# Attention projections by eights: queries of eight heads in one beat, their keys in the next, with the batch's preparation further ahead

## The chip, the cores and the metric

The kernel runs on one core of a Trainium2 chip (trn2). Its engines are TensorE (PE), VectorE (DVE), ScalarE (ACT), GpSimd (POOL) and SyncE (SP), which issues most of the DMAs. The metric is the device time of one execution in microseconds, the median of three runs. One further execution was profiled; all rows below come from it.

## The reference, cut to what matters

Sixteen batches of 256 rows with 128 features pass through one layer: layer norm, then attention and a mixture of experts side by side, both added to the input.

```python
xn = layernorm(x)                                   # (16, 256, 128)
kv_c = rms(xn @ W_kv) * g_kv;  q_c = xn @ W_q       # ranks 32 and 64
q = concat(heads(q_c @ W_qdec), rope(heads(q_c @ W_qrope)))    # 16 heads of 8 + 32
k = concat(heads(kv_c @ W_kdec), rope(heads(xn @ W_krope)))
v = heads(kv_c @ W_vdec)
attn = softmax(causal(q @ k.T / sqrt(40)))
y = (attn @ v) @ W_o
probs = softmax(xn @ Wg)                            # 8 experts, two per row
moe = sum over the two picked e of weight * (silu(xn @ W1[e] + b1[e]) @ W2[e] + b2[e])
shared = 0.1 * (silu(xn @ Ws1 + bs1) @ Ws2 + bs2)
out = x + y + moe + shared
```

## The kernel before, in words

The order of the work is written out by hand. Each engine runs its own copy of the same loop over beats t and four steps s (`beats`, line 466), from FIRST = -5 to LAST = 71. A group g is four heads of a batch (HG = 4, PER = 4 groups to a batch, NG = 64 groups), and beat t starts group t. What an engine does in a step is decided by lags: `project(t)` in step 0, the transposes ("turnings") of its parts from one to two beats later (`TURN_AT`, line 48), scores for the maximum three beats later, the negated maxima four, the scores for the softmax five, values six. Engines wait for each other through semaphores only, and every queue is in order.

One beat, in its parts:

- `project(g)` on TensorE (line 1411) fills both banks of the tensor "projections": for each of the two row tiles j two matmuls of 160 columns for the queries of four heads (lines 1428, 1429), three of 128 columns for the rope part of the keys (1433 to 1435) and two of 32 columns for key content and values (1436, 1437): 14 matmuls. Before it, it waits for the preparation of the beat before, since that uses the same banks.
- `rotate(g)` on VectorE (1034) multiplies by the cosine table and makes two products with the sine table (1038, 1042, 1043); `add_turned` on GpSimd (693, line 697) adds them; `part_heads` on ScalarE (820, line 825) writes the high part twice; `take_low` on GpSimd (699, line 702) the low part.
- `turn_parted` (1441, line 1448) turns the parts in four units of four transposes; `put_stack` copies each unit to QK, on VectorE for i = 1 (1050) and on ScalarE otherwise (802).
- `scores_for_max` (1452, lines 1461 to 1464), `head_max` on VectorE (1057), `negative_max` on VectorE (1060, lines 1067, 1071, 1073), `turn_maxima` on TensorE (1473), `put_max` on ScalarE (810), `place_maxima`, a DMA of SyncE's queue (521).
- `head_scores` (1477), `exponential` on ScalarE (796), `group_values` (1490); per pair of groups `turn_pair` and `norm_pair`, per batch the output projection.

Scores for the maximum, transposes, maxima and outputs share a ring of three PSUM banks; the units' order (`units_at`, 98) fixes which bank each takes, and TensorE may fill a unit only when the one three places before it was read.

A batch's preparation runs in four of the beats ahead of its first group: `normalise` (beat -5 relative to it), `turn_rows` and its copies (-4), `small_rows` and `small_products` (-3), `small_stacks` (-2), `turn_stacks` and its copies (-1). TensorE's parts stand at the end of step 2, ScalarE's copies in step 3 behind part_heads (lines 857, 862, 867, 868), VectorE's share (lines 1308, 1011 to 1021, 1027 to 1032) in steps 2 and 3. The router works on four batches at a time (`ROUTE_AT`), its rows are scattered to expert order by GpSimd's indirect DMAs (`scatters_at`, line 740), and `list_blocks` on VectorE (1167) lists the expert blocks in the last beats. SyncE meanwhile zeroes free rows (`fill`, 542) and loads the shared weights (`load_shared`, 552). Behind the beats follow 31 passes of experts (`hidden`, `activate`, `expert_out`); the first two and the last six are the shared expert's, and the third is the first that turns routed rows (1590).

```python
                if s == 3 and group(t):
                    part_heads(t)
                b = batch_at(t, -4)
                if s == 3 and b is not None:
                    ...
                    act_f(xhl[:, b % 2, 0, :], banks[0][:, 0:T], ACT.Copy).then_inc(s_xh, 1)
```

## Time and profile before

| What | us |
|---|---|
| median of 3 runs | 987.04 |
| lowest and highest run | 982.11, 991.94 |
| the profiled execution | 989.52 |
| its span in the profile | 987.8 |

The span runs from the first to the last recorded instruction; what lies around it is in the execution's own time. In the profile's rows an engine's name is followed by the line of the kernel, the operation, and output<-input. PE is TensorE's matmuls and PEld its weight loads, which overlap them. "PEclk" is the granted TensorE clock as a share of full speed, a mean over the window. "x4" after a row stands for four instructions merged into one. A name in angle brackets tells what ended an idle time.

### The profile page before, as it was taken

How to read it: one execution, taken by the hardware profiler on the slowest of the kernel's cores; microseconds unless marked ns; L12 is line 12 of the kernel's file. 1: busy time of each engine (PE TensorE's matmuls, PEld its weight loads, DVE VectorE, ACT ScalarE, POOL GpSimd, SP SyncE). 2: the span in 40 equal slices, each digit the busy share in tenths (PEclk: the TensorE clock that was granted, in tenths of full speed). 3: DMA queues.
4: the chain of work that ended last, by engine and by line, in shares of the span. 5: the costliest groups of instructions: out<-in, count | busy, mean ns of one | idle time of the engine just before them, and what ended most of it. 6: DMA issues, size and time to landing. Idle time of an engine off the chain costs nothing.

```text
span 987.8 us, 17323 instructions
## 1 busy us (share of the span) xinstructions
PE 796.4 (81%) x5926; PEld 691.3 (70%) x5926; DVE 636.4 (64%) x1546; ACT 512.6 (52%) x1006; POOL 385.0 (39%) x346
## 2 busy tenths in 40 slices
PE   2688888888878788887888888789556999988974
PEld 2677787777768677776777777687444888876863
DVE  4456577665747876565777657469565777765775
ACT  2335454545654454555546456556334777765562
POOL 3534333445545454434434334334610000246544
PEclk9999777778978897888879789778866999998988
DMA  6020211102020211100011100000234477877643
GB/s 177 12 76 1 76 41 37 57 31 82 7 84 7 82 53 38 61 7 21 7 39 42 39 18 8 21 7 11 76 109 148 141 243 245 247 220 231 210 120 83
DMA packets 51557, 79.43 MB, mean 80 GB/s; under 512 B 5889, under 2 KB 31470, under 8 KB 51470
## 3 DMA queue, kind: packets, MB, share of 16 engines
q1 hardware_dynamic: 46798, 69.23, 22.1%
q0 software_dynamic: 4096, 8.40, 2.9%
q8 instruction: 49, 0.80, 0.4%
q10 hardware_dynamic: 576, 0.69, 0.2%
q14 instruction: 38, 0.31, 0.1%
HBM read 47.82 MB, written 29.88 MB: 79 GB/s over the span
## 4 chain that ended last, share of the span: by engine, by line
PE 59%; DVE 15%; ACT 9%; issue 8%; another core or an unknown queue 3%; POOL 2%; DMA 2%; SPq 1%; ACTq 0%; POOLq 0%; DVEq 0%
PE bank L1448 7%; ACT heads_parted L825 5%; PE bank L1670 5%; PE projections L1608 4%; PE bank L1608 4%; PE bank L1484 4%; PE bank L1498 3%; PE bank L1487 3%; PE bank L1464 3%; PE bank L1461 3%; PE bank L1674 2%; PE projections L1428 2%; POOL QK L758 2%; PE projections L1433 2%
## 5 line engine op out<-in xcount | busy, mean ns | idle before, releaser
L1057 DVE TENSOR_REDUCE mx<-bank 128x3 f32<-128x384 f32 x256 | 141.9, 555 | 106.7 <-PE bank L1464 86.1
L697 POOL TENSOR_TENSOR rot<-rot,t 128x512 f32<-128x512 f32 x64 | 82.0, 1282 | 269.3 <-DVE t L1043 269.3
L796 ACT ACTIVATE prob<-bank 128x384 f32<-128x384 f32 x256 | 125.8, 492 | 91.2 <-PE bank L1487 80.4
L1448 PE MATMUL bank<-identr,heads_parted 128*120 128x128 f32 x1024 | 158.4, 289 | 8.9 <-DVE mx L1057 7.2
L802 ACT ACTIVATE QK<-bank 120x512 fp32r<-120x512 f32 x192 | 115.0, 599 | 61.0 <-PE bank L1448 53.8
L758 POOL DMA_INDIRECT QK<-expert_outs,out_at x64 | 67.6, 1056 | 190.4 <-DMA expert_outs<-prob 166.9
L702 POOL TENSOR_TENSOR heads_parted<-rot,heads_parted 128x640 fp32r<-128x640 f32 x64 | 98.9, 1545 | 96.5 <-ACT heads_parted L825 96.1
L1448 PEld LDWEIGHTS bank<-identr,heads_parted 128*120 128x120 f32 x1024 | 126.6, 159 | 11.3 <-DVE mx L1057 6.9
L810 ACT ACTIVATE mT<-bank 8x256 fp32r<-8x256 f32 x64 | 23.8, 372 | 206.3 <-PE bank L1473 195.8
L1461 PE MATMUL bank<-QK 120*128 120x256 f32 x256 | 110.5, 432 | 8.2 <-ACT mT L810 6.6
L1357 DVE TENSOR_TENSOR QK<-vaug,QK 128x512 fp32r<-128x512 f32 x124 | 85.5, 695 | 46.8 <-ACT QK L910 37.6
L1484 PE MATMUL bank<-QK 122*128 122x256 f32 x256 | 105.3, 411 | 4.5 <-DMA QK<-mT 4.5
L1428 PE MATMUL projections<-wqa,qsT 128*128 128x160 f32 x128 | 38.3, 321 | 85.3 <-DVE wb L1308 30.0
L1050 DVE CAST QK<-bank 120x512 fp32r<-120x512 f32 x64 | 44.0, 688 | 78.3 <-PE bank L1448 76.6
L1428 PEld LDWEIGHTS projections<-wqa,qsT 128*128 128x128 f32 x128 | 26.8, 210 | 93.8 <-issue 65.3
L1487 PE MATMUL bank<-identb,mask_qk 128*128 128x256 bf16 x256 | 85.7, 335 | 0.0
L1464 PE MATMUL bank<-mask_qk,identb 128*128 128x256 bf16 x256 | 85.2, 333 | 0.0
L825 ACT ACTIVATE heads_parted<-rot 128x1280 fp32r<-128x1280 f32 x64 | 80.8, 1263 | 1.8 <-POOL rot L697 1.8
L1461 PEld LDWEIGHTS bank<-QK 120*128 120x128 f32 x256 | 64.1, 250 | 10.5 <-ACT mT L810 6.8
L740 POOL DMA_INDIRECT expert_rows<-xn,place_of x64 | 65.5, 1023 | 12.6 <-issue 11.8
L1484 PEld LDWEIGHTS bank<-QK 122*128 122x128 f32 x256 | 59.1, 231 | 8.8 <-DMA QK<-mT 4.7
L1462 PE MATMUL bank<-QK 120*128 120x128 f32 x256 | 64.2, 251 | 0.0
(227 smaller groups left out, 2038.2 us busy)
## 6 DMA issues: line engine op xcount, KB each, us to landing
...
```

The costliest lines, as they stand in the source:

```text
L702: nc.gpsimd.tensor_tensor(low_of(g), rotated(g), high_of(g), ALU.subtract).then_inc(s_lo, 1)
L758: nc.gpsimd.indirect_dma_start(out=gy[:, t, k, :], out_offset=None, in_=outs_d[0:READY[q] * SLOTS, :], in_offset=bass.IndirectOffsetOnAxis ...
L796: act_f(prob[:, g % 2 * HG + n, :], ST_PS[n % 2][:, 0:3 * P], ACT.Exp, scale=SCALE).then_inc(s_exp, 1)
L802: act_f(stacked(g, i), B_PS[bank_of(k)][0:KQ, :].rearrange("p (h t) -> p h t", h=HG), ACT.Copy)\
L825: act_f(high_of(g, 2), rotated(g).unsqueeze(3).to_broadcast([P, 2, NT * HG, 2, D]), ACT.Copy).then_inc(s_hi, 1)
L1057: V.tensor_reduce(mx[:, 0:3, g % 2 * HG + n], B_PS[bank_of(k)][:, 0:3 * P].rearrange("p (a c) -> p a c", a=3), AX.X, ALU.max).then_inc(s_b ...
L1357: V.tensor_tensor(aparts[:, m % 2, 1, c, :], act[c], high, ALU.subtract).then_inc(s_alo, 1)
L1448: ins = nc.tensor.transpose(B_PS[bank_of(k)][0:KQ, n * P:(n + 1) * P].bitcast(F32R), parted(g, i, n), identr[:, :])
L1461: mm(ps[:, 0:T], q[:, P:T], kk, start=True, stop=False, skip_group_check=True)
L1464: mm(diag, identb[:, :], mask_qk[:, :].unsqueeze(1).to_broadcast([P, 2, P]), start=False, stop=True, skip_group_check=True).then_inc(s_bfi ...
L1484: mm(ps[:, P:3 * P], k[:, 0:P], q, start=True, stop=False, skip_group_check=True)
L1487: mm(diag, mask_qk[:, :], identb[:, :].unsqueeze(1).to_broadcast([P, 2, P]), start=False, stop=True, skip_group_check=True).then_inc(s_st, 1)
```

## The change

A beat now projects one side for eight heads. Beat g with g even makes the queries of the eight heads of groups g and g+1, beat g+1 their keys and values. `PH` is 8; the rotation works on two tiles of eight heads and not on four of four heads; the parts of queries (high, high, low) and keys (low, high, high) are laid out by the parity of g. Scores need both beats, so they start at step 14 behind a group's beat and not 12, the maxima at 18 and not 16, the scores for the softmax at 22 and not 20, the values half a beat later. A batch's preparation is moved to beats -7, -6, -4, -3 and -2, its TensorE parts all in beats of queries (even beats), with a third slot for the batch's rows and a second for its turned keys. On ScalarE the copies of the preparation go ahead of the stack copies in step 3, and part_heads to step 0 of the next beat. On VectorE the rotation is split around the maxima. On GpSimd take_low goes to step 1, the scatters to step 0 and two beats earlier, with waits on the scores from beat 63 on; the weight splits to step 3. In the last beats the shared loads are split over beats 66 and 68, the fills of free rows follow them, and the listing's last part goes to the fourth expert pass. The first expert's hidden layer starts two beats ahead of the last beat and not one.

```diff
-OS = 2 * T // 2
-ROW = HG * D
-MAX_LAG, NEG_LAG, SC_LAG, PV_LAG = 3, 4, 5, 6
+PH = 2 * HG
+ROW = PH * D
+MAX_AT, NEG_AT, SC_AT = 14, 18, 22
 TURN_AT = {3: (1, 0), 0: (2, 1), 1: (2, 2), 2: (2, 3)}
-FIRST, LAST = -5, NG + 7
-HL_SLOTS = 3
-HL_SIDE = 1040
-HL_SLOT = 2000
-P_SLOTS = 2 * HG
+FIRST, LAST = -7, NG + 7
+HL_SLOTS, X_SLOTS, P_SLOTS = 3, 3, 2 * HG
+HL_SLOT = NT * PH * KQ
...
+def staged(t, s, at):
+
+    g, n = divmod(STEPS * t + s - at, HG)
+    return (g, n) if group(g) else (None, n)
...
+def values_at(t, s):
+
+    if s == 0 and group(t - 7) and (t - 7) % 2 == 0:
+        return t - 7
+    if s == 2 and group(t - 6) and (t - 6) % 2 == 1:
+        return t - 6
...
-ROUTE_AT = {0: (10, 3), 1: (11, 3), 2: (12, 2), 3: (12, 3), 4: (13, 2), 5: (14, 0), 6: (14, 3)}
-POS_AT = 14
+ROUTE_AT = {0: (9, 2), 1: (10, 1), 2: (10, 3), 3: (11, 1), 4: (11, 3), 6: (12, 3), 5: (13, 2)}
+EXP_AT, POS_AT = 10, 12
...
-    if 15 <= t < 63:
-        return (t - 15) // 16, ((t - 15) % 16,)
-    if 63 <= t < 71:
-        return GROUPS - 1, (2 * (t - 63), 2 * (t - 63) + 1)
+    if 13 <= t < 61:
+        return (t - 13) // 16, ((t - 13) % 16,)
+    if 61 <= t < 69:
+        return GROUPS - 1, (2 * (t - 61), 2 * (t - 61) + 1)
...
+                if (t, s) == (66, 0):
+                    load_shared(0)
+                if (t, s) == (68, 0):
+                    load_shared(1)
+                    sp.wait_ge(s_free, 1)
+                    for i in range(E):
                         fill(sp.value_load(fill_row[0:1, i:i + 1], min_val=0, max_val=ROWS - SLOTS))
...
-                if s == 0 and group(t - 1):
+                if s == 1 and group(t - 1):
                     take_low(t - 1)
...
+                q, picks = scatters_at(t) if s == 0 else (None, ())
                 for pick in picks:
+                    if t >= 63:
+                        pool.wait_ge(s_st, STEPS * t - SC_AT + 2 * (pick % 2))
...
+                first = 8 * (g % PER // 2)
+                for odd in range(2):
+                    act_f(vaug[:, g // PER % V_SLOTS, :, first + odd:first + PH:2, 2 * DC * odd:2 * DC * odd + DC],
+                          prs[:, :, ROW:ROW + PH * DC].rearrange("p j (n a d) -> p j n a d", a=2, d=DC)[:, :, :, odd, :],
+                          ACT.Copy).then_inc(s_v, 1)
...
+                g, n = staged(t, s, SC_AT)
+                if g is not None:
+                    exponential(g, n)
+                b = batch_at(t, -6)
+                if s == 3 and b is not None:
+                    sc.wait_ge(s_afill, rows_turned(b))
+                    at_least(sc, s_xst[b % X_SLOTS], 16 * (b // X_SLOTS))
+                    at_least(sc, s_pfill, PER * (b - X_SLOTS + 1))
+                    act_f(xhl[b % X_SLOTS][:, 0, :], banks[0][:, 0:T], ACT.Copy).then_inc(s_xh, 1)
+                b = batch_at(t, -4)
+                if s == 3 and b is not None:
+                    sc.wait_ge(s_afill, small_done(b))
+                    at_least(sc, s_small, b)
+                    act_f(smt[:, :, :], banks[1][:, :].rearrange("p (j c) -> p j c", j=NT)[:, :, 0:SMW],
+                          ACT.Copy).then_inc(s_smh, 1)
+                b = batch_at(t, -2)
+                if s == 3 and b is not None:
+                    sc.wait_ge(s_afill, stacks_turned(b))
+                    at_least(sc, s_pfill, PER * b - 1)
+                    act_f(qsT[:, :, :], banks[1][:, 0:T].rearrange("p (j t) -> p j t", j=NT), ACT.Copy).then_inc(s_smT, 1)
+                    act_f(ksT[b % 2][:, :, :], banks[1][0:3 * RKV, T:2 * T].rearrange("p (j t) -> p j t", j=NT),
+                          ACT.Copy).then_inc(s_smT, 1)
+                if s == 0 and group(t - 1):
+                    part_heads(t - 1)
                 lag, i = TURN_AT[s]
                 if group(t - lag) and i != 1:
                     put_stack(t - lag, i)
-                if s == 2 and group(t):
+                if s == 2 and group(t) and t % 2:
                     read_values(t)
-                if s == 1 and pair_at(t) is not None:
+                if s == 3 and pair_at(t) is not None:
                     pair = pair_at(t)
...
+                if s == 1 and group(t):
+                    rotate(t)
+                g = begun(t, s, NEG_AT)
+                if g is not None:
+                    negative_max(g)
...
+                g, n = staged(t, s, MAX_AT)
+                if g is not None:
+                    head_max(g, n)
+                if s == 1 and group(t):
+                    rotate_turned(t)
+                lag, i = TURN_AT[s]
+                if group(t - lag) and i == 1:
+                    put_stack(t - lag, i)
...
+                if m == 3:
+                    next(listing, None)
...
+                b, first = g // PER, 8 * (g % PER // 2)
+                heads = slice(first, first + PH)
                 at_least(pe, s_turned, g)
-                at_least(pe, s_v, g)
-                x_next, s_next = batch_at(g - 1, -4), batch_at(g - 1, -3)
-                if x_next is not None:
-                    pe.wait_ge(s_xl, x_next + 1)
-                if s_next is not None:
-                    pe.wait_ge(c_a, s_next * SMALL_STEPS + 7)
+                at_least(pe, s_v, g // 2 * 2)
+                b_x, b_s, b_k = (batch_at(g - 1, beat) for beat in (-6, -4, -2))
+                if b_x is not None:
+                    pe.wait_ge(s_xl, b_x + 1)
+                if b_s is not None:
+                    pe.wait_ge(c_a, b_s * SMALL_STEPS + 7)
+                if b_k is not None:
+                    pe.wait_ge(s_smT, 2 * (b_k + 1))
+                if g == 0:
+                    pe.wait_ge(s_smT, 2)
+                    pe.wait_ge(s_xl, 2)
                 if group_at(g - 1, POS_AT) is not None:
                     pe.wait_ge(s_posr, group_at(g - 1, POS_AT) + 1)
                 for j in range(NT):
                     ps = prs[:, j, 0:ROW]
-                    mm(ps, qsT[:, j, :], wqa[:, heads, :], start=True, stop=False, skip_group_check=True)
-                    mm(ps, qsT[:, j, :], wqb[:, heads, :], start=False, stop=True, skip_group_check=True)
-                for j in range(NT):
-                    ps = prs[:, NT + j, 0:ROW].rearrange("p (h d) -> p h d", d=D)
-                    xh, xl = (xhl[:, b % 2, a, j * P:(j + 1) * P] for a in range(2))
+                    if g % 2 == 0:
+                        mm(ps, qsT[:, j, :], wqa[:, heads, :], start=True, stop=False, skip_group_check=True)
+                        ins = mm(ps, qsT[:, j, :], wqb[:, heads, :], start=False, stop=True, skip_group_check=True)
+                        continue
+                    ps = ps.rearrange("p (h d) -> p h d", d=D)
+                    xh, xl = (xhl[b % X_SLOTS][:, a, j * P:(j + 1) * P] for a in range(2))
                     mm(ps[:, :, DC:D], xh, wkr[:, 0, heads, :], start=True, stop=False, skip_group_check=True)
                     mm(ps[:, :, DC:D], xh, wkr[:, 1, heads, :], start=False, stop=False, skip_group_check=True)
                     mm(ps[:, :, DC:D], xl, wkr[:, 0, heads, :], start=False, stop=True, skip_group_check=True)
-                    mm(ps[:, :, 0:DC], ksT[:, j, :], wkv[:, 0, heads, :], start=True, stop=True, skip_group_check=True)
-                    ins = mm(prs[:, NT + j, ROW:ROW + HG * DC], ksT[:, j, :], wkv[:, 1, heads, :],
+                    mm(ps[:, :, 0:DC], ksT[b % 2][:, j, :], wkv[:, 0, heads, :], start=True, stop=True, skip_group_check=True)
+                    ins = mm(prs[:, j, ROW:ROW + PH * DC], ksT[b % 2][:, j, :], wkv[:, 1, heads, :],
                              start=True, stop=True, skip_group_check=True)
                 ins.then_inc(s_pfill, 1)
...
-                if s == 0 and group(t):
-                    project(t)
+                g, n = staged(t, s, SC_AT)
+                if g is not None:
+                    head_scores(g, n)
+                g, n = staged(t, s, MAX_AT)
+                if g is not None:
+                    scores_for_max(g, n)
                 lag, i = TURN_AT[s]
                 if group(t - lag):
                     turn_parted(t - lag, i)
-                g = t - PV_LAG
-                if group(g) and s == (0 if g % 2 else 2):
-                    group_values(g)
-                if s == 0 and group(t - NEG_LAG):
-                    turn_maxima(t - NEG_LAG)
-                if s == 2 and pair_at(t) is not None:
-                    turn_pair(pair_at(t))
+                if values_at(t, s) is not None:
+                    group_values(values_at(t, s))
+                if s == 0 and group(t):
+                    project(t)
+                g = begun(t, s, NEG_AT)
+                if g is not None:
+                    turn_maxima(g)
                 if s == 1 and out_batch(t) is not None:
                     turn_normed(out_batch(t))
+                if s == 2:
+                    if batch_at(t, -2) is not None:
+                        turn_stacks(batch_at(t, -2), t)
+                    if batch_at(t, -4) is not None:
+                        small_rows(batch_at(t, -4), t)
+                    if batch_at(t, -6) is not None:
+                        turn_rows(batch_at(t, -6), t)
+                    if group_at(t, POS_AT) is not None:
+                        count_places(group_at(t, POS_AT), t)
+                if s == 3 and pair_at(t) is not None:
+                    turn_pair(pair_at(t))
                 if s == 3 and out_batch(t) is not None:
                     output_projection(out_batch(t))
-                if s == 2:
-                    if batch_at(t, -4) is not None:
-                        turn_rows(batch_at(t, -4), t)
-                    if batch_at(t, -3) is not None:
-                        small_rows(batch_at(t, -3), t)
-                    if batch_at(t, -1) is not None:
-                        turn_stacks(batch_at(t, -1), t)
-                    if group_at(t, POS_AT) is not None:
-                        count_places(group_at(t, POS_AT), t)
-                if (t, s) == (LAST - 1, 0):
+                if (t, s) == (LAST - 2, 0):
```

The parts left out change the slices with the slots (`parted`, `high_of`, `low_of`, `stacked`), count the fillings of the preparation's banks, and make the cosine and sine tables for eight heads. GpSimd's two powers and SyncE's store of the rows follow the preparation's new beats.

## Rows read from the trace of the kernel before

**Rows 1.** The page, part 1: busy time and share of each engine.
```profile
PE 796.4 (81%) x5926; PEld 691.3 (70%) x5926; DVE 636.4 (64%) x1546; ACT 512.6 (52%) x1006; POOL 385.0 (39%) x346
```

**Rows 2.** Windows: busy us (instructions) of each engine, PEclk, DMA share, GB/s.
```profile
302.00:696.00 394.00, 325.92 (x2890) 289.91 (x2890) 263.13 (x688) 208.93 (x436) 166.35 (x137) 0.85 0.09 29
696.00:761.10 65.10, 36.27 (x278) 27.42 (x278) 36.05 (x79) 21.61 (x46) 18.23 (x18) 0.71 0.38 122
761.10:987.80 226.70, 201.45 (x949) 163.14 (x947) 156.61 (x304) 142.41 (x238) 67.56 (x64) 0.95 0.62 191
```

**Rows 3.** VectorE's rotation, line 1038: durations min/median/max, first and last start.
```profile
L1038 DVE TENSOR_TENSOR rot<-projections,rope_table x64: 811/814/825, 22.0 to 696.0; 128x640 f32<-128x640 f32 x64
```

**Rows 4.** Waits from 302 to 696: us in total, times, longest.
```profile
PE projections L1428 <- DVE wb L1308: 15.9, 8, 2.0
PE projections L1428 <- DVE smt L1011: 15.7, 8, 2.0
PE projections L1428 <- ACT ksT L868: 15.3, 9, 1.7
```

**Rows 5.** Timeline, all engines, from 454.6: start, us, what, [idle before <-releaser].
```profile
454.65 0.98 POOL L740 DMA_INDIRECT expert_rows<-xn,place_of  x1 [0.15 <-issue]
...
455.10 1.26 ACT L825 ACTIVATE heads_parted<-rot 128x1280 fp32r<-128x1280 f32 x1
456.25 0.38 ACT L857 ACTIVATE wb<-projections 128x256 fp32r<-128x256 f32 x1
456.45 1.54 POOL L702 TENSOR_TENSOR heads_parted<-rot,heads_parted 128x640 fp32r<-128x640 f32 x1 [0.82 <-ACT heads_parted L825]
456.52 0.49 ACT L796 ACTIVATE prob<-bank 128x384 f32<-128x384 f32 x1
456.66 0.42 DVE L1308 TENSOR_TENSOR wb<-projections,wb 128x256 fp32r<-128x256 f32 x1 [1.78 <-ACT wb L857]
...
457.23 0.31 PE L1428 MATMUL projections<-wqa,qsT 128*128 128x160 f32 x1 [1.99 <-DVE wb L1308]
```

**Rows 6.** Windows behind the idle time of rows 5, and near 708.
```profile
457.20:462.80 5.60, 5.57 (x43) 4.64 (x43) 2.31 (x5) 0.55 (x2) 0.79 (x1) 0.58 0.14 47
706.00:709.00 3.00, 1.87 (x27) 1.31 (x26) 1.33 (x3) 0.00 (x0) 2.39 (x3) 1.00 0.39 119
```

**Rows 7.** Timeline of TensorE from 480.09: scores, then one projection, then four turnings.
```profile
480.09 0.36 PE L1461 MATMUL bank<-QK 120*128 120x256 f32 x1
480.30 0.22 PE L1462 MATMUL bank<-QK 120*128 120x128 f32 x1
...
480.40 0.32 PE L1428 MATMUL projections<-wqa,qsT 128*128 128x160 f32 x1
...
481.97 0.52 PE L1448 MATMUL bank<-identr,heads_parted 128*120 128x128 f32 x4
```

**Rows 8.** Windows: two beats, each from one rotation to the next.
```profile
474.90:485.10 10.20, 9.78 (x98) 8.34 (x96) 6.82 (x19) 5.72 (x13) 3.91 (x3) 0.82 0.03 9
485.10:494.80 9.70, 7.54 (x62) 7.00 (x61) 6.96 (x25) 5.79 (x14) 4.59 (x4) 0.87 0.02 8
```

**Rows 9.** Lines 1071 and 697: durations in ns min/median/max, first and last start.
```profile
L1071 DVE TENSOR_SCALAR nhl<-mx x64: 170/172/1575, 51.4 to 737.0; 128x8 fp32r<-128x8 f32 x64
...
L697 POOL TENSOR_TENSOR rot<-rot,t x64: 1262/1282/1297, 23.6 to 697.5; 128x512 f32<-128x512 f32 x64
```

**Rows 10.** Timeline of VectorE near 19: the normalised rows of batch 1.
```profile
19.02 0.60 DVE L1002 TENSOR_SCALAR xn<-xres,mv,rstd 128x128 f32<-128x128 f32 x2 [0.44 <-POOL rstd L722]
```

**Rows 11.** The chain that ended last, from 708 to 766: start, us, what.
```profile
708.81 14.43 another core or an unknown queue
...
738.16 5.99 DMA QK<-mT
...
746.63 2.46 issue
```

**Rows 12.** The first long operation of the listing's last part.
```profile
L1269 DVE TENSOR_TENSOR xn<-xn 128x2048 f32<-128x2048 f32 x1 | 2.3, 2292 | 0.0
```

249 lines of the change are left out of this document (110 added, 139 removed).

## The prediction, made before the change was run

> **What bounds the kernel now.** I read the page's engine line first, then the windows by stage, then the waits, then the timeline. The page shows TensorE busiest at 81% and VectorE at 64% [rows 1]; neither is full, so the end is set by how they wait for each other. The windows divide the span [rows 2]: beats up to the last rotation at 696.0, the last beats to the first turning of routed rows at 761.1, then 226.7 us of experts, in which TensorE is busy 201.45 us and of which the change touches one place.
>
> The rotation runs once per beat, 64 times from 22.0 to 696.0, so 63 beats take 674.0 us, 10.70 each [rows 3]. The window from 302 to 696 holds 394/10.70 = 37 of them, 10.65 us each. Per such beat the window gives TensorE 325.92/37 = 8.81 us busy, VectorE 263.13/37 = 7.11, ScalarE 5.65, GpSimd 4.50, at a granted clock of 0.85 [rows 2].
>
> In three beats of four TensorE stands still before `project`: 15.9 + 15.7 + 15.3 = 46.9 us in 25 waits, 1.88 us each, 1.27 per beat over 37 [rows 4]. The timeline shows why: ScalarE starts part_heads (1.26 us) at 455.10, copies the batch's rows behind it at 456.25, VectorE subtracts at 456.66, and TensorE, idle since about 455.24, projects at 457.23 [rows 5]. The wait is paid twice: in the 5.6 us behind it the granted clock is 0.58, mostly the lower level of 1.2 GHz, whereas from 706 to 709, with TensorE busy only 1.87 of 3 us, it is still 1.00, that is 2.4 GHz [rows 6].
>
> **The change part by part.**
> (1) Preparation ahead of part_heads. ScalarE's copies of rows, small products and turned stacks now stand directly behind the exponential of step 3, and part_heads goes to step 0 of the next beat. `project` also moves behind the turning of step 0 and, in even beats, the values. Between the preparation's matmuls and the next `project` lie now two steps of score and turning work; three matmuls of scores take 0.31 us, twice a step, four turnings 0.4 to 0.5 [rows 7], about 1 us a step at full clock. The chain that must fit is ScalarE's exponential 0.49, copy 0.38, VectorE 0.42 [rows 5], about 1.5 us with hand-overs. It fits, so I take the whole 1.27 us per beat as gone (bounds: 0 and 1.27).
> (2) The clock. 0.85 means that 30% of the 394 us, 118 us, ran at half clock. At full clock the busy part (83%) of that would take half: 49 us less, 1.3 per beat. Bounds: 0, if other waits of the same size come, and 1.3.
> (3) Wide projections. A beat's 14 matmuls start between 480.40 and 481.97, 0.112 us apart whatever their width, so two beats cost 3.14 us; 256 columns take 0.21 [rows 7]. Afterwards two beats issue 4 of 320 columns, 6 of 256 and 4 of 64. With every one at 0.112 that is 1.57 us; with the wide ones at 0.22, 0.21 and the narrow at 0.112, 2.59. I take 2.0, nearer the per-instruction price since 128 and 160 columns showed no difference: 0.57 us less per beat (0.28 to 0.79).
> TensorE's side of a beat would be 10.65 - 1.27 - 1.3 - 0.57 = 7.5 us.
> (4) VectorE keeps all its work: one rotation of 640 and two products of 256 elements per partition, the same maxima, the same preparation in larger lumps. Its 7.11 us per beat now weigh as much as TensorE. It cannot be full: rotate stands first in step 1 and waits for a later `project`. The two windows between rotations give the price of such coupling: from 485.1 to 494.8 took 9.7 us with VectorE busy 6.96; without the 1.7 us wait for the stacks 8.0, 1.04 above its busy time [rows 4, 8]. So 7.11 + 1.04 = 8.15.
> (5) negative_max moves from step 0 to step 2, directly behind the products whose end starts GpSimd's sum of 1.28 us. Its small operations are sometimes held: L1071 has a median of 172 ns and a maximum of 1575 [rows 9]. TensorE's turn_maxima and the maxima behind wait for it. I add 0.35 us per beat (bounds 0 and 1.3) and come to 8.5 us.
> The Trainium skill bears on this (SBUF — State Buffer, "Who interferes with whom"): VectorE and GpSimd share one port pair, and a VectorE operation with two SBUF inputs waits out a GpSimd operation that reads SBUF and came first. The maximum of 1575 ns agrees with a lock held for a whole GpSimd operation. It speaks against the new place of negative_max; what it would do is rival 2.
> (6) Same cost, other place: read_values becomes two ScalarE copies in every second beat, each of the old size; the second ksT and third x slot cost no instruction; the router's parts and the scatters come one to two beats earlier; take_low is now behind the scatter on GpSimd, which puts 0.98 us of descriptor work ahead of it [rows 5], and ahead of add_turned. GpSimd has 6.1 us free per beat of 10.65, 4.0 of 8.5. From the part copy (1.26) and take_low (1.54) to the turning in step 3 some 5 us of TensorE's steps remain against 2.8 plus the exponential of step 0. I cost it at nothing; rival 4 is its exposure.
> (7) Start. Batch 1's rows are now prepared ahead of the first `project`. Before, its xn came only at 19.02 [rows 10], 3 us ahead of the first rotation; now it, its turning, copy and subtraction stand in front of ScalarE's copies for that projection: at most the 3 us, half of it made good by a shorter first projection: +1.5 (0 to 3).
> (8) Last beats. 65.1 us from 696.0 to 761.1. The chain there has one piece of 14.43 us put to an unknown queue, 5.99 of the maxima's rows landing, 2.46 before the values [rows 11]. In the first, GpSimd issued its last scatters without a pause (two per beat in the program, but nothing held them); the rows' DMA started in the midst of 2 MB of loads; the third waited behind the listing on VectorE. The change paces the scatters by the scores, starts the loads at beats 66 and 68 around the last place_maxima, moves the listing's last part away, and lets TensorE start the first expert's hidden layer a beat earlier in place of a wait. I take off 14.4, 4.0 (2 us is a transfer's own) and 2.5, and add 3 for the half beat by which scores and values come later: 47.2 us. Fills, loads and rows behind beat 68 are about 4.5 MB; at the experts' stage rate of 191 GB/s over a share of 0.62, 308 GB/s, 15 us, from about 27 us on: 42, just inside. Bounds for the stretch: 40 and 65.
> (9) The listing's last part, three operations like L1269 with 2.29 us and some small ones, 7.5 us [rows 12], now falls into expert pass 3. VectorE is busy 156.61 of 226.7 us there, 2.0 us free per pass of 6.5; I take 3 us exposed (0 to 7.5).
>
> **Sum.** First rotation 22.0 + 1.5 = 23.5; eight first beats at 9.5 us (clock and pipeline still filling) 76; 55 at 8.5, 467.5: last rotation at 567.0, 129 us earlier. Then 47.2, 226.7 and 3: a span of 843.9. The profiled execution lasted 989.52 for its span of 987.8, 1.7 more, and 2.5 above the median 987.04; so 843.9 + 1.7 - 2.5 = 843 us.
>
> **The rivals.**
> 1. VectorE and TensorE overlap better than the old windows show: 7.5 us a beat, the sum of (1) to (3). 55 us less: 788. For it: TensorE no longer stops; against: VectorE would have 95% of the beat.
> 2. The port. GpSimd's sum is released by the same products that negative_max follows, so its three small operations wait about 1.28 us each beat, TensorE's turn_maxima with them, and part of the clock loss returns: 9.4 us a beat, 50 more: 893. For it rows 9; against: the first small operation is in before GpSimd starts, and in the old order most were not held.
> 3. The waits were only one of several causes. From 474.9 to 485.1, a beat with no such wait, still took 10.2 us at a clock of 0.82 [rows 8]. If beats stay at 9.9, 77 more: 920. Against: that low clock was left by the wait before it.
> 4. Slower than before: the later part_heads. If ScalarE's burst in step 3 and GpSimd's scatter and weight splits push take_low past the turning of step 3, TensorE waits each beat. Exposed by half, 1.4 us, and the clock falling as in rows 6 (5.6 us at 0.58, some 2.4 us lost): 3.8 us a beat, 209 more: 1052. It decides from 144/55 = 2.6 us per beat.
> 5. The change doesn't do what it says: the wide matmuls cost per column what two narrow ones did, and the preparation's wait only moves to the next queue: within 1% of before.
>
> **How the numbers follow.** Forecast (beats of 7.9 to 9.1 us, 810 to 876) 0.55; rival 1 0.13; rival 2 0.18; rival 3 0.07; rival 4 0.04; rival 5 0.03. The range of 8 in 10 takes the forecast, the nearer part of rival 1 and rival 2 with a longer tail of last beats: 800 to 915. Faster by over 1%, about what a measurement of this kernel can tell from none: 0.93; within 1%: 0.03; slower: 0.04.
>
> **What would show it.** (1) right: no idle of over 1 us before the first projection line, wrong if the row copy on ScalarE still ends behind it. (2) a granted clock of 0.95 or more over the steady beats. (3) four matmuls of 320 columns starting about 0.15 us apart. (4) rotations 8.5 us apart and VectorE busy over 80% of such a window. (5) the median of what is now L1071 near its 172 ns; a median over a microsecond is rival 2. (8) under 50 us from the last rotation to the first turning of expert rows, and no 14 us piece. (9) one gap of about 3 us in pass 3 or 4. The prediction is wrong if GpSimd's chain shows as TensorE's longest wait at the turning, or the clock stays at 0.85.

## The result, and the profile after

The changed kernel takes 916.69 us (median of four, 907.99 to 919.31), the kernel before 989.49 in the same set: a ratio of 0.9259, 95% interval 0.9176 to 0.9343. That is 7.4% faster. The forecast was 843 us, range 800 to 915. Half of the forecast gain came. Ratios here and below are computed from the executions in the faster of two states, so they are not exactly the quotients of the medians. The profiled execution of the changed kernel took 915.65 us for a span of 913.9.

The page, part 1, of the changed kernel, to be held against [rows 1]:

```profile
PE 712.7 (78%) x5478; PEld 618.1 (68%) x5478; DVE 664.2 (73%) x1546; ACT 514.7 (56%) x1006; POOL 384.9 (42%) x346
```

TensorE is busy 84 us less with 448 fewer matmuls. VectorE, with not one instruction more (1546 as before), is busy 28 us longer: some of its instructions got slower. This is the first sign of the cause.

The windows and the rotation answer to [rows 2] and [rows 3]; the columns are as there.

```profile
235.00:630.20 395.20, 305.26 (x2873) 273.15 (x2871) 295.33 (x736) 230.29 (x476) 184.09 (x154) 0.89 0.11 35
630.20:690.70 60.50, 41.83 (x320) 33.77 (x320) 33.08 (x76) 25.21 (x53) 14.89 (x14) 0.75 0.34 109
690.70:913.90 223.20, 201.71 (x948) 162.96 (x948) 164.43 (x313) 141.57 (x237) 68.37 (x64) 0.96 0.64 198
```
```profile
L1083 DVE TENSOR_TENSOR rot<-projections,rope_table x64: 809/824/826, 25.6 to 630.2; 128x640 f32<-128x640 f32 x64
```

Read: 604.6 us for 63 beats, 9.60 each (before 10.70; forecast 8.5 after the first eight). The last beats, up to the first turning of routed rows, take 60.5 us (before 65.1, forecast 47.2), the experts 223.2 (before 226.7, forecast 229.7). Against the forecast the last rotation is 63.2 us late, the last beats are 13.3 us longer and the experts 6.5 shorter: the span of 913.9 misses 843.9 by 70. A steady beat has 305.26/41.2 = 7.4 us of TensorE, so TensorE stands still for 2.2 us, and VectorE has 295.33/41.2 = 7.2.

What TensorE waits for in that window, longest first (us, times, longest), where [rows 4] had three waits ahead of `project`:

```profile
PE bank L1534 <- DVE nhl L1121: 62.9, 40, 3.3
PE bank L1570 <- ACT heads_out L909: 18.3, 19, 1.0
PE bank L1522 <- DVE mx L1105: 4.2, 8, 0.5
```

The waits ahead of `project` are gone. In their place stands one ahead of turn_maxima (L1534), 1.57 us in every beat, and one ahead of turn_pair (L1570), 0.96 in every second. The timeline shows the first one being made:

```profile
455.17 0.41 DVE L1091 TENSOR_TENSOR t<-projections,rope_table 128x256 f32<-128x256 f32 x1
455.50 0.15 DVE L1115 TENSOR_TENSOR mx<-mx 128x4 f32<-128x4 f32 x1
455.66 1.26 POOL L733 TENSOR_TENSOR rot<-rot,t 128x512 f32<-128x512 f32 x1 [1.00 <-DVE t L1091]
455.69 1.26 DVE L1119 TENSOR_SCALAR nhl<-mx 128x8 fp32r<-128x8 f32 x1
456.98 0.17 DVE L1121 SCALAR_TENSOR_TENSOR nhl<-mx,nhl 128x8 fp32r<-128x8 f32 x1
...
457.20 0.38 PE L1534 MATMUL bank<-identr,nhl 128*8 128x128 f32 x2 [1.63 <-DVE nhl L1121]
```

VectorE's products end and release GpSimd's sum (L733). L1119, the second instruction of negative_max and eight elements wide, starts 0.03 us behind the sum and ends with it. The sources of the two lines, for [rows 9]:

```profile
L1119 DVE TENSOR_SCALAR nhl<-mx x64: 171/1265/1282, 51.7 to 669.0; 128x8 fp32r<-128x8 f32 x64
```
```profile
L733 POOL TENSOR_TENSOR rot<-rot,t x64: 1253/1272/1386, 27.2 to 633.3; 128x512 f32<-128x512 f32 x64
```

The median went from 172 to 1265 ns, the length of the sum. In 41 of the 64 beats L1119 took over a microsecond, and each time it ended within 0.1 us of the sum. In 14 of the other 23 it was normalised (L1046) that ended with the sum, and negative_max came behind it; TensorE waited for negative_max in all 64 beats, 104.5 us in total. And as in [rows 6], the idle time is paid twice: the window behind it shows TensorE full at the lower level (columns as in the windows):

```profile
457.20:460.20 3.00, 3.00 (x24) 2.90 (x24) 0.42 (x1) 0.92 (x3) 0.00 (x0) 0.51 0.08 24
```

### The profile page after: what moved, and what is told of

The parts are those of the page before. It is cut to its first block, busy times and chain, and to the rows that moved or that the text cites. A ratio compares the mean times of both kernels' runs of the same rounds, so it can differ in the third digit from the quotient of the medians.

```text
span 913.9 us, 16429 instructions
## 1 busy us (share of the span) xinstructions
PE 712.7 (78%) x5478; PEld 618.1 (68%) x5478; DVE 664.2 (73%) x1546; ACT 514.7 (56%) x1006; POOL 384.9 (42%) x346
## 4 chain that ended last, share of the span: by engine, by line
PE 50%; DVE 31%; issue 8%; ACT 3%; another core or an unknown queue 2%; POOL 2%; SPq 1%; DMA 1%; ACTq 1%; POOLq 0%; DVEq 0%
DVE nhl L1119 6%; PE bank L1507 4%; PE bank L1732 4%; DVE mx L1105 4%; PE projections L1668 4%; PE bank L1668 4%; DVE rot L1083 3%; PE bank L1545 3%; DVE t L1091 3%; DVE xn L1046 3%; PE bank L1522 3%; DVE nhl L1121 3%; PE bank L1525 3%; PE bank L1548 3%
## 5 line engine op out<-in xcount | busy, mean ns | idle before, releaser
L1105 DVE TENSOR_REDUCE mx<-bank 128x3 f32<-128x384 f32 x256 | 141.9, 554 | 109.1 <-PE bank L1525 108.5
L738 POOL TENSOR_TENSOR heads_parted<-rot,heads_parted 128x640 fp32r<-128x640 f32 x64 | 99.5, 1555 | 138.7 <-ACT heads_parted L865 138.1
L1507 PE MATMUL bank<-identr,heads_parted 128*120 128x128 f32 x1024 | 151.1, 279 | 5.5 <-DVE mx L1105 4.0
L1507 PEld LDWEIGHTS bank<-identr,heads_parted 128*120 128x120 f32 x1024 | 121.4, 153 | 9.7 <-DVE mx L1105 7.0
L1522 PE MATMUL bank<-QK 120*128 120x256 f32 x256 | 106.6, 417 | 4.2 <-DVE mx L1105 4.2
L733 POOL TENSOR_TENSOR rot<-rot,t 128x512 f32<-128x512 f32 x64 | 82.0, 1281 | 61.5 <-DVE t L1091 61.3
L1545 PE MATMUL bank<-QK 122*128 122x256 f32 x256 | 101.3, 396 | 0.4 <-ACT prob L834 0.4
L1534 PE MATMUL bank<-identr,nhl 128*8 128x128 f32 x128 | 19.1, 233 | 104.5 <-DVE nhl L1121 104.5
L1534 PEld LDWEIGHTS bank<-identr,nhl 128*8 128x8 f32 x128 | 7.1, 83 | 117.6 <-DVE nhl L1121 117.6
L1525 PE MATMUL bank<-mask_qk,identb 128*128 128x256 bf16 x256 | 82.6, 323 | 0.0
L1083 DVE TENSOR_TENSOR rot<-projections,rope_table 128x640 f32<-128x640 f32 x64 | 52.6, 821 | 34.9 <-PE projections L1495 33.0
L1522 PEld LDWEIGHTS bank<-QK 120*128 120x128 f32 x256 | 61.3, 239 | 6.1 <-ACT QK L840 4.8
L1546 PE MATMUL bank<-QK 122*128 122x128 f32 x256 | 63.0, 246 | 0.0
```

The costliest lines, as they stand in the source:

```text
L733: nc.gpsimd.tensor_tensor(rope_part, rope_part, t2[g % 2][:, :, :], ALU.add).then_inc(s_rot, 1)
L738: nc.gpsimd.tensor_tensor(low_of(g), rotated(g), high_of(g)[:, :, 0:D], ALU.subtract).then_inc(s_lo, 1)
L1105: V.tensor_reduce(mx[:, 0:3, g % 2 * HG + n], B_PS[bank_of(k)][:, 0:3 * P].rearrange("p (a c) -> p a c", a=3), AX.X, ALU.max).then_inc(s_b ...
L1507: ins = nc.tensor.transpose(B_PS[bank_of(k)][0:KQ, n * P:(n + 1) * P].bitcast(F32R), parted(g)[:, j * PH + 2 * n + odd, :], identr[:, :])
L1522: mm(ps[:, 0:T], q[:, P:T], kk, start=True, stop=False, skip_group_check=True)
L1525: mm(diag, identb[:, :], mask_qk[:, :].unsqueeze(1).to_broadcast([P, 2, P]), start=False, stop=True, skip_group_check=True).then_inc(s_bfi ...
```

## The experiments

All kernels below are edits of the changed kernel. They ran in five sets, on different chips; the kernel before took 988.9, 983.4, 949.0, 952.4 and 952.7 us in them, so ratios are compared within a set. Across sets the last rotation serves: it was at 630.2 us in both profiled executions of the changed kernel, on chips where its time was 916.7 and 895.0. Equal kernels differed by about 2 us in it elsewhere (e5 and e16; e7, whose beats are the changed kernel's). Each last rotation is from one profiled execution.

| set | kernel | last rotation, us | time, us | ratio to before |
|---|---|---|---|---|
| - | before | 696.0 | 989.49 | 1 |
| - | changed | 630.2 | 916.69 | 0.9259 |
| 1 | e1 negative_max earlier | 590.8 | 877.14 | 0.8882 |
| 1 | e2 other form | 626.8 | 915.00 | 0.9203 |
| 1 | e3 turn_maxima later | 646.1 | 935.67 | 0.9464 |
| 1 | e4 turn_pair later | 599.4 | 889.06 | 0.9006 |
| 2 | e5 e1 and e4 | 585.3 | 869.65 | 0.8863 |
| 2 | e6 narrow projections | 670.8 | 963.21 | 0.9841 |
| 2 | e7 biases in pass 0 | 632.4 | 917.58 | 0.9327 |
| 2 | e8 part_heads first | 705.4 | 1002.54 | 1.0222 |
| 3 | e9 preparation moved | 607.9 | 876.68 | 0.9216 |
| 3 | e10 biases and fills | 631.5 | 895.47 | 0.9396 |
| 3 | e11 all edits | 593.1 | 858.16 | 0.9033 |
| 3 | e12 no sum beside | 544.9 | 810.86 | 0.8532 |
| 4 | e13 changed again | 630.2 | 894.98 | 0.9397 |
| 4 | e14 e11 mended | 584.7 | 849.59 | 0.8922 |
| 4 | e15 sum in quarters | 596.4 | 866.77 | 0.9099 |
| 4 | e16 e5 again | 583.1 | 849.77 | 0.8918 |
| 5 | e17 e5, sum in quarters | 563.0 | 829.86 | 0.8715 |
| 5 | e18 and take_low in quarters | 572.0 | 838.29 | 0.8798 |

The intervals of the ratios are 0.004 to 0.009 to either side.

**Who holds negative_max: e1, e2, e12, e15.**

```diff
 # e1: in head_max's place, and no longer at the start of step 2
                     head_max(g, n)
+                    if n == HG - 1:
+                        negative_max(g)
```


> The changed kernel with one edit: VectorE's negative_max comes in step 1, right behind the fourth head_max, ahead of rotate_turned; GpSimd's add_turned, which waits for rotate_turned, can then not run beside it. Theory (the missing 1.1 us per beat is the second instruction of negative_max held beside GpSimd's sum, 1265 ns for a median of 172 before, with TensorE's turn_maxima waiting 1.63 us for it in each of 64 beats and the half clock behind it): this instruction falls below 200 ns, the wait ahead of turn_maxima below 0.3 us per beat, the beat to 8.5 to 8.8 us and the time to 850 to 870 us. Rival (the beat is set by VectorE's own sum of work or by the ring of banks, and the wait is only where it shows): the held instruction goes, the beat stays at 9.4 to 9.6 us, the time at 905 to 920.

```diff
 # e2
-V.tensor_scalar(nhl[:, g % 2, :, 0, :], mx[:, 2:4, heads], -1.0, None, ALU.mult)
+V.scalar_tensor_tensor(out=nhl[:, g % 2, :, 0, :], in0=mx[:, 2:4, heads], scalar=-1.0,
+                       in1=unit[:, 0:HG]..., op0=ALU.mult, op1=ALU.mult)
```


> The changed kernel with negative_max left in its place (step 2, behind rotate_turned) and its second instruction written as a scalar_tensor_tensor (times -1, times a tile of ones) in place of a tensor_scalar; same values. Theory, in its sharper form (it is the form of the instruction that is held beside GpSimd's sum, since L1115 and L1121 in other forms took 154 and 168 ns at the median in the same places): it falls to about 170 to 200 ns, the beat to 8.5 to 9.0 us, the time to 855 to 885. Rival (whatever VectorE issues beside GpSimd's sum is held until it ends): it stays at about 1.2 us, the time at 910 to 920.

```diff
 # e12: GpSimd's sum cut to one of 16 parts
-tensor_tensor(rope_part, rope_part, t2[g % 2][:, :, :], ALU.add)
+tensor_tensor(rope_part[:, 0:1, :], rope_part[:, 0:1, :], t2[g % 2][:, 0:1, :], ALU.add)
```


> The changed kernel with GpSimd's add_turned cut to the first of its 16 groups of elements per partition (the rest of the sum is left out); order and waits are unchanged, negative_max stands in step 2. If it is GpSimd's sum that holds VectorE's instruction: L1119 falls to its 170 ns in the very place where it took 1265, the wait ahead of turn_maxima from 1.63 to about 0.5 us per beat, the time to 860 to 885 (GpSimd's chain is shorter too). If it is the place itself (pipeline behind the products, the semaphore): L1119 stays over 1 us.

```diff
 # e15: the same sum in four instructions
+for n in range(4):
+    at = slice(4 * n, 4 * n + 4)
+    ins = tensor_tensor(rope_part[:, at, :], rope_part[:, at, :], t2[g % 2][:, at, :], ALU.add)
```


> The changed kernel with GpSimd's add_turned issued as four instructions of 128 elements per partition (32 elements took 251 ns in e12, 512 take 1281, so about 0.45 us each and 1.8 in all, 0.5 more than now). If VectorE's instruction is held for one GpSimd instruction at a time and gets in between two, L1119 falls from 1265 to 300 to 500 ns, the wait ahead of turn_maxima by 0.7 us a beat, the time to 885 to 905 on the first chip's scale (ratio 0.90 to 0.92). If it is held until GpSimd's run of instructions ends, L1119 takes 1.6 to 1.8 us and the ratio is 0.93 to 0.95.

The instruction in question, by its source, in e2, e12 and e15, and GpSimd's quarter in e15:

```profile
L1119 DVE SCALAR_TENSOR_TENSOR nhl<-mx,unit x64: 166/1260/1281, 51.6 to 665.7; 128x8 fp32r<-128x8 f32 x64
```
```profile
L1119 DVE TENSOR_SCALAR nhl<-mx x64: 170/180/256, 50.1 to 580.5; 128x8 fp32r<-128x8 f32 x64
```
```profile
L1122 DVE TENSOR_SCALAR nhl<-mx x64: 170/455/971, 51.5 to 633.6; 128x8 fp32r<-128x8 f32 x64
...
L735 POOL TENSOR_TENSOR rot<-rot,t x256: 442/454/632, 27.2 to 600.8; 128x128 f32<-128x128 f32 x128
```

In its old place but without a long sum beside it, it takes 180 ns (e12): not the place, the sum is the cause. (e12 leaves out 15 of the sum's 16 parts.) With the sum in quarters it takes 455 ns, a quarter's 454: in all 50 beats in which it was held, VectorE was held for the one GpSimd instruction under way and got in behind it. The instruction behind it, L1121 in the changed kernel (168 ns at the median) and L1124 here, then waits for a further quarter:

```profile
L1124 DVE SCALAR_TENSOR_TENSOR nhl<-mx,nhl x64: 166/371/379, 51.9 to 633.8; 128x8 fp32r<-128x8 f32 x64
```

But VectorE does not get in between two GpSimd instructions every time. In the changed kernel, behind the last rotation, the four-element L1115 took 2.54 us, to the end of take_low and of the whole sum that follows it without a gap:

```profile
631.80 1.55 POOL L738 TENSOR_TENSOR heads_parted<-rot,heads_parted 128x640 fp32r<-128x640 f32 x1
632.05 2.54 DVE L1115 TENSOR_TENSOR mx<-mx 128x4 f32<-128x4 f32 x1
633.30 1.26 POOL L733 TENSOR_TENSOR rot<-rot,t 128x512 f32<-128x512 f32 x1
```

What decides between the two cases is not shown.

The other form changed nothing (1260): my sharper reading, that only the form of L1119 is held, is refuted. L1115 had been at 154 ns because it started before the sum, not for its form; placed beside take_low in e1 it was held as well:

```profile
468.20 1.57 POOL L738 TENSOR_TENSOR heads_parted<-rot,heads_parted 128x640 fp32r<-128x640 f32 x1
```
```profile
468.43 0.55 DVE L1105 TENSOR_REDUCE mx<-bank 128x3 f32<-128x384 f32 x1
469.12 0.68 DVE L1115 TENSOR_TENSOR mx<-mx 128x4 f32<-128x4 f32 x1
469.83 0.17 DVE L1119 TENSOR_SCALAR nhl<-mx 128x8 fp32r<-128x8 f32 x1
```

L1115 ends with L738, at 469.8, while L1105, which reads PSUM, passes beside L738 in its usual 0.55. With the sum nearly gone TensorE still waits for negative_max in 45 beats of e12, so a part of the wait in the changed kernel is not the sum's hold. What is left in e12 is the later place, behind rotate and rotate_turned, and in 15 beats L1121 beside GpSimd's weight split, where it takes up to 1108 ns:

```profile
PE bank L1534 <- DVE nhl L1121: 44.5, 45, 2.4
```

In price: e1 takes 39.4 us off the last rotation (0.63 per beat), e15 33.8 although GpSimd works 0.5 us longer, e12 85.3 (1.35 per beat, its shorter GpSimd chain included). e1 fell between both of its expectations: its wait ahead of turn_maxima is down to 6.0 us in all, as the theory had it, but the beat is 8.97 us for 8.5 to 8.8 and the time 877.14 for 850 to 870. Waits for single maxima (24.2 and 19.7 us) and for the copy oT (14.8) have come up in its place. e12 gained more than expected (0.853 of the kernel before, for the 0.87 to 0.89 that 860 to 885 us were on the first chip); e15 came as its theory said.

**Where TensorE asks: e3 and e4.**

```diff
 # e3: turn_maxima in units and on TensorE     # e4: turn_pair on TensorE
-g = begun(t, s, NEG_AT)                      -if s == 3 and pair_at(t) is not None:
+g = begun(t, s, NEG_AT + 1)                  +if s == 0 and pair_at(t - 1) is not None:
```


> The changed kernel with TensorE's turn_maxima one step later (step 3 in place of 2), nothing else moved: VectorE's instruction stays held, TensorE asks for it about 2 us later. If the price is TensorE's wait and the clock behind it: no wait of note ahead of turn_maxima, beat 8.5 to 8.9 us, time 855 to 880. If the held 1.1 us of VectorE is itself what the beat pays: beat 9.2 to 9.6, time 895 to 920. A turning this late can also make head_scores wait for the rows of maxima: then it shows as a wait on the DMA ahead of head_scores.

> The changed kernel with turn_pair moved from the end of step 3 to step 0 of the next beat, behind the scores; it waited 28.7 us over 31 times for ScalarE's copy heads_out. Theory (waits of TensorE in a bound near 9.6 us are paid in full, with half clock behind them): 28.7 us less and some clock, 885 to 900 us. Rival (the wait is made good by the next wait, for negative_max in the same beat): 910 to 920.

e3 falls out of both expectations: it is slower than the changed kernel (646.1, 935.67). TensorE no longer waits for negative_max, but for banks of the ring instead, and longer for heads_out:

```profile
PE bank L1507 <- DVE mx L1105: 54.9, 53, 3.1
PE bank L1570 <- ACT heads_out L909: 48.3, 32, 1.6
PE projections L1598 <- DVE xn L1046: 24.4, 16, 13.1
PE bank L1507 <- ACT QK L840: 14.9, 17, 1.4
PE bank L1522 <- ACT QK L840: 13.5, 13, 1.3
```

L1119 is held as before (1284 ns at the median). My reading is that VectorE's lateness shows in whichever wait comes next. It was not tested by itself: the edit also moves turn_maxima in the order in which units take the ring's banks, and that alone could bring the new waits. e4 came as the theory said, at its lower end: 30.8 us off the last rotation (27.6 off the time) for a wait of 28.7 us that shrank to 6.7, with the page's clock at 0.928 for 0.886. The wait for negative_max took back little of it (111.3 us in all for 104.5).

**Together: e5.** 

> The changed kernel with both edits that gained: negative_max ahead of rotate_turned (alone 877.14, ratio 0.8882) and turn_pair in step 0 of the next beat (alone 889.06, ratio 0.9006). If the two waits are separate prices, each paid in full, 39.6 and 27.6 us come off 916.7: 849, within 842 to 858, the beat at 8.5 us, which is the beat that was forecast. Rival (they share their cover: one wait's end is made good by the other): not under 865.

The rival's kind of answer: 585.3, only 45 us earlier than the changed kernel where the single edits gave 39.4 + 30.8. So the two prices are not added up; that they share cover is the reading that fits. The forecast beat was not reached: 8.88.

**What the other steps are worth: e6 and e8.**

```diff
 # e6: each of project's matmuls as two, of four heads each (160, 128 and 32 columns)
+for n in range(2):
+    hs = slice(first + HG * n, first + HG * (n + 1))
 # e8: on ScalarE in step 3
+                    put_stack(t - 1, 0)
+                    part_heads(t)        # ahead of the preparation's copies, as before the change
```


> The changed kernel with each matmul of project split in two halves of its columns (160, 128 and 32 in place of 320, 256 and 64): 28 matmuls in two beats in place of 14, the same sums. It prices step (3) of the prediction, 0.57 us per beat: if TensorE's instructions are paid in full, 36 us more, 945 to 960, and bounds of 18 to 50 us. Rival (the projections stand between waits, which shrink by what they grow): 915 to 925.

> The changed kernel with ScalarE's part_heads put back to where it stood before the change: step 3 of its own beat, behind put_stack and ahead of the preparation's copies. Step (1) of the prediction says that this order cost 1.27 us of TensorE per beat. If the order on ScalarE is what took the waits away: a wait of about 1.3 us ahead of project or of the small matmuls comes back in three beats of four, 960 to 1000 us. Rival (it is project's own place behind the turning and the values, and the copies' head start of whole beats, that took them away): 905 to 925, with no such wait; the earlier part_heads could even gain.

e6: the last rotation is 40.6 us later, 0.64 per beat, the time 45.6 over e7's (whose beats are the changed kernel's). 963.21 is a little above the 945 to 960 that I expected, and the cost is inside the bounds of 18 to 50. e8: 75.2 us later, 1.19 per beat, and slower than the kernel before; 1002.54 is at the upper end of what I expected. But its waits are not those that I expected:

```profile
PE bank L1536 <- DVE nhl L1123: 111.1, 64, 3.7
PE bank L1572 <- ACT heads_out L911: 63.2, 32, 2.1
...
PE projections L1493 <- DVE smt L1057: 12.7, 12, 2.2
PE projections L1493 <- ACT ksT L900: 8.6, 13, 2.3
```

Only 21.3 us of these stand ahead of `project` (26.5 with three waits for the router's rank); the larger part is turn_pair, now 2.0 us in every second beat, since ScalarE's copy heads_out has part_heads ahead of it. The kernel before had no such wait in its list, as its turn_pair came a step behind the copy. So without the new order on ScalarE nothing of the change's gain is left, but e8 is not the old wait put back.

**The last beats: e7, e10, and the kernels of all edits, e11 and e14.**

```diff
 # e7, e10: the part of the listing that waits for the last scatter
-if 64 <= t < 68 and s in (1, 3):      +if ... and (t, s) != (67, 3):
-if m == 3:                            +if m in (0, 3):
 # e10: the fills, one per beat
+if s == 0 and 61 <= t < 69:
+    fill(sp.value_load(fill_row[0:1, t - 61:t - 60], ...))
```


> The changed kernel with the listing's part that picks the blocks' biases (it waits for the last scatter to land: VectorE idle 7.46 us in the last beats, norm_pair and so the last values of TensorE behind it) moved from step 3 of beat 67 to the start of expert pass 0. Theory (the tail's missing 13 us are in part this wait): the last beats 4 to 8 us shorter, 908 to 913 us. Rival (SyncE's queue of fills, weights and rows, from 670.1 to 686.6, ends last anyway): the same within 2 us, 915 to 918.

> The changed kernel with the biases' part in pass 0, as in e7, and with the eight fills one per beat in beats 61 to 68 instead of all behind beat 68. In e7 the last beats ended on SyncE's queue instead (TensorE 4.65 us idle for the rows, 10.40 us of fills ahead of them). Theory (two chains end nearly together there, VectorE's wait for the scatter and SyncE's fills, and only both edits shorten the stretch): from the last rotation to the first turning of rows 52 to 56 us in place of 60.5, 909 to 913 us. Rival (the last scatter's landing at about 677 us and the rows' transfer behind it end last anyway, or the fills get in the way of the maxima's rows): 59 to 61, no gain.

In the changed kernel VectorE stood 7.46 us in front of L1301 for the last scatter, with norm_pair behind it. In e7 this is gone, and TensorE waits for the routed rows instead, behind ten microseconds of fills on SyncE:

```profile
676.81 0.92 DVE L1301 TENSOR_REDUCE xn<-xn 128x92 f32<-128x736 f32 x1 [7.46 <-DMA expert_rows<-xn,place_of]
```
```profile
674.54 10.40 SPq L578 DMA_DIRECT2D expert_rows<-zeros  x8
```
```profile
692.22 1.09 PE L1650 MATMUL bank<-ident,rot 128*128 128x128 f32 x4 [4.65 <-DMA rot<-expert_rows]
```

The first line is the changed kernel's, the others e7's. e7 leaves the stretch at 59.8 and the time at 917.58, as its rival said. Both edits give 56.8 (e10), just above the 52 to 56 expected, and the time of e10 is that of the changed kernel (895.47 and 894.98, on two chips where the kernel before took 949.0 and 952.4). Four microseconds are too few to show between sets. The fills alone were not run.

```diff
 # e9: e5, and on VectorE                   # e11: e9, e10, and ScalarE's copy oT in step 1
-s == 1 ... normalised    +s == 0, last      # e14: e11 with normalised left in step 1
-s == 2 ... small_stacks  +s == 3
```


> The kernel of e5_negmax_and_pair (869.65, ratio 0.8863) with the two other groups of VectorE's SBUF-only instructions that stood beside GpSimd's sum moved away from it: normalised (two at 0.77 us each behind rotate_turned) to the end of step 0, small_stacks (L1072 held for 1.06 us) to step 3; the router's first part waits for the logits alone instead of small_stacks. Theory (what is left above the forecast beat of 8.5 is again VectorE held beside GpSimd, once per batch and place, with TensorE waiting for bank and maxima behind it: 24.7 + 20.8 us): 10 to 25 us less, 845 to 860. Rival (the beat of 8.9 is now the ring of banks and the clock): 865 to 872 with the held instructions gone.

> All edits in one kernel: negative_max ahead of rotate_turned, turn_pair in step 0 of the next beat, normalised and small_stacks clear of GpSimd's sum, the biases' part in pass 0, the fills one per beat, and ScalarE's copy oT at the end of step 1 instead of step 2 (turn_maxima waited 14.8 us in 14 beats for it). If these are prices of their own: the steps of e9 and e10 and half of the 14.8 add up, 835 to 850 us, about what was forecast for the change itself. Rival (they share cover, as the first two did): 855 to 868.

> e11 without its one bad move: normalised stays behind rotate_turned (moved to the end of step 0 it ran beside GpSimd's take_low instead and two took 2.49 us at 455.77 in e9). So: negative_max ahead of rotate_turned, turn_pair in step 0, small_stacks in step 3, copy oT in step 1, biases' part in pass 0, fills one per beat. Theory: the edits of the tail are worth 4 us (60.5 to 56.4 in e10), small_stacks and the copy up to 10: 8 to 16 us under e16_both_again, ratio 0.87 to 0.88. Rival: small_stacks in step 3 stands ahead of head_max's and put_stack's successors as normalised did, and nothing is gained over e16.

e9 also lets the router's first part wait for less. It went the wrong way: 607.9, 23 us behind e5. I had moved normalised clear of the sum and into the scatter's issue and take_low:

```profile
455.77 2.49 DVE L1046 TENSOR_SCALAR xn<-xres,mv,rstd 128x128 f32<-128x128 f32 x2
```
```profile
455.30 1.03 POOL L778 DMA_INDIRECT expert_rows<-xn,place_of  x1 [0.20 <-issue]
456.37 1.54 POOL L738 TENSOR_TENSOR heads_parted<-rot,heads_parted 128x640 fp32r<-128x640 f32 x1
```

Two instructions that took 1.55 us together beside the sum take 2.49, with rotate behind them. That move is not the whole of the 23 us: e11, which keeps it, has its last rotation at 593.1, and e14, which differs from e11 in this move alone, at 584.7, 8.4 us earlier. What the rest of e9's loss is, and what the copy oT made good of it in e11, was not tried apart. e11 is at 0.9033 of the kernel before, so behind e5's 0.8863. e14 is level with e5's kernel in the same set (849.59 and 849.77) and misses its 0.87 to 0.88: small_stacks, the copy and the tail together bring nothing that can be measured in the time, though the last beats are shorter (54.1 us for 59.4 in e16).

**References, and what holds the rest: e13, e16, e17, e18.**

> The changed kernel itself, unedited, beside e14_best, e15_sum_in_quarters and e16_both_again. In the runs e9 to e12 the kernel before took 948.96 us against 988.92 and 983.37 in the two sets ahead of them, so times of different sets can't be subtracted. Expected: 0.926 of the kernel before, whatever that takes here.

> The kernel of e5_negmax_and_pair again, as the reference for e14 in this set. Expected: 0.957 of e13_changed_again (0.8863 over 0.9259), within 0.01.

> The kernel of e16_both_again (ratio 0.8918) with add_turned in four instructions, as in e15. What stands beside the sum there is head_max, normalised (907 ns each) and small_stacks (955 ns for its first), not negative_max. If holds of normalised and small_stacks still price the beat: they fall by half and the ratio to 0.875 to 0.885. If the sum's 0.5 us more on GpSimd, which part_heads waits for, weighs more: 0.89 to 0.90.

> As e17, and take_low in four instructions too; L1115, the first of negative_max, now stands beside take_low and took 446 ns at the mean in e16 for 161 unheld. If that hold is what is left of the port: L1115's mean under 250 ns and 0.005 to 0.015 less than e17 in the ratio. If take_low's later end (about 0.5 us) makes TensorE wait at the turning of step 3: more than e17.

e13 came out at 0.9397 of before (interval 0.9335 to 0.9458), above the 0.926 of the first set and of its expectation; e16 at 0.949 of e13 for 0.957 expected. e17 is better than hoped. The holds of normalised and small_stacks, in e16 and then in e17:

```profile
L1046 DVE TENSOR_SCALAR xn<-xres,mv,rstd x32: 334/874/2661, 10.3 to 508.2; 128x128 f32<-128x128 f32 x32
...
L1072 DVE TENSOR_TENSOR smt<-smt,rs x16: 212/1060/1062, 18.8 to 534.5; 128x64 f32<-128x64 f32 x16
```
```profile
L1049 DVE TENSOR_SCALAR xn<-xres,mv,rstd x32: 335/478/2660, 10.3 to 491.9; 128x128 f32<-128x128 f32 x32
...
L1075 DVE TENSOR_TENSOR smt<-smt,rs x16: 214/230/240, 18.8 to 516.7; 128x64 f32<-128x64 f32 x16
```

By the groups of lines, the first went from 904 to 586 ns at the mean (32 of them, 10.2 us), the second from 955 to 231 (16, 11.6 us): 21.8 us of VectorE. The other two instructions of small_stacks take 11.7 us less. The last rotation comes 20.1 us earlier, at 563.0; that it is so near the 21.8 is chance as far as the runs show. The beat is 8.53 us, the forecast's 8.5. e17 is 829.86 us, 0.8715 of the kernel before (0.8663 to 0.8767), the best that ran. e18 lost 9 us of that again: at the mean L1115's successor stayed at 473 ns (476 in e17), take_low became 0.55 us longer, and L1119's went from 192 to 296. Which of these the loss is was not tried.

## Why the prediction was right or wrong

The prediction failed in the beat, put at 8.5 us and measured at 9.60: in step (5), which priced a hold too low, and in step (6), which left a wait out.

**(1) right:** all three waits of [rows 4] are gone. e8 gives 1.19 us per beat for the order on ScalarE and I had 1.27, but that is in part chance, since the larger part of e8's waits is for heads_out.

**(2) wrong in its condition.** The clock was to go to full once the waits were gone; it is 0.89. New waits came, which the step had named as its lower bound. In e12 the window up to the last rotation shows 0.96, in e17 0.93.

**(3) right:** 0.64 us per beat in e6 for 0.57 forecast. The sign is there too: at full clock the matmuls of 320 columns start 0.15 us apart.

```profile
471.61 0.31 PE L1487 MATMUL projections<-wqb,qsT 128*128 128x320 f32 x1
471.76 0.31 PE L1486 MATMUL projections<-wqa,qsT 128*128 128x320 f32 x1
```

**(4) the size fits, the reason is not shown.** VectorE's beat with coupling was put at 8.15, and 8.24 is the beat of e12, in which GpSimd's sum is nearly gone. But that VectorE sets this beat does not follow. In e12 it is busy 75% of the time and TensorE 83% (columns as in the windows), and 6.2 us a beat for my 7.11. The old kernel's 7.11 had holds by GpSimd in it already, which I took for work: of 64 times, L1071 took over 0.3 us in 10 and L1067, the first of negative_max, in 17.

```profile
235.00:544.90 309.90, 256.97 (x2618) 229.02 (x2616) 232.80 (x676) 208.12 (x433) 128.95 (x139) 0.96 0.11 37
```

**(5) is the step that failed.** "I add 0.35 us per beat (bounds 0 and 1.3)". I judged from [rows 9] that the instruction is sometimes held, where the new order releases the sum directly ahead of it. It was held to the sum's end in 41 beats of 64, and in 14 of the others normalised, ahead of it, was. The edit that undoes it is worth 0.63 us per beat (e1), still inside my bounds; the sum's absence is worth 1.35 (e12), with GpSimd's shorter chain in it. So the mechanism was named, and its price was put too low. It is rival 2 ("9.4 us a beat"): the beat is 9.60, and the changed kernel's time of 917 lies 24 us from its 893; I gave it 0.18. The argument against it, that most were not held in the old order, spoke of an order in which GpSimd's sum was not released just there.

The rule of the Trainium skill that I cited (SBUF — State Buffer, "Who interferes with whom") is of VectorE operations with two SBUF inputs. It covers L1115, L1121 and e2's form of L1119, which took 1260 ns. L1119 itself has one SBUF input, so the cited rule does not cover it. What the page says further of VectorE instructions in a two-port mode, which it allows to tensor_scalar, does: whoever issues first has the shared pair for the whole instruction. The 1265 ns agree, and so do e15's 455; the 2.54 us above, over two GpSimd instructions, are more than that sentence says. That an instruction with a PSUM source and one SBUF source stays clear of it agrees with L1090 and L1091, which never took over 418 ns in 64 beats each, 40 of the 128 beside take_low.

**(6) wrong by an omission.** "Same cost, other place" left turn_pair out: before, a step lay between the values, ScalarE's copy and the turning; now copy and turning stand in the same step. 28.7 us of wait, 30.8 us of beats (e4), costed at nothing. Together with (5) it is 45 us (e5) of the 63 by which the last rotation missed 567.0. The first rotation has 2 more; the other 16 are not assigned. e17, which also shortens the holds of normalised and small_stacks, is past them, at 563.0.

**(7)** First rotation at 25.6 for 23.5, 3.6 us later than before and so just outside the 0 to 3 us.

**(8) mis-sized:** 60.5 for 47.2. The 14 us piece is gone as forecast, but I took each removed piece off as if nothing ended close behind it. Two chains did: VectorE's 7.46 us for the scatter and SyncE's fills; negative_max was held there also (the 2.54 us above), and the clock was 0.75. How the 13.3 us divide among these is open: removing both chains gave 3.7 (e10).

**(9) right:** one gap, behind the listing's last part on VectorE, for 3 us forecast:

```profile
719.58 0.64 PE L1650 MATMUL bank<-ident,rot 128*128 128x128 f32 x4 [3.41 <-DVE heads_parted L1396]
```

Rivals 1, 4 and 5 did not come about: the beat never went to 7.5, a wait at the turning for GpSimd's chain is at most 0.7 us in the list, and both halves of the change pay. Rival 3's number, 920, is nearer to 916.69 than any other. Its reason, that beats stay slow without a wait, is not what the trace shows: the beats lost time to two new waits, and with one or the other of them smaller the clock rose (e12, e4). That the beat is at 8.5 in e17 and not below is not explained further: 20.8 and 15.0 us of waits for maxima and 14.8 for the copy oT are left, and none of them was taken away by itself.
